# Silu as ScalarE's own function in a fused Mamba and MLP kernel, with a new table of slots

## The reference, cut to what matters

```python
# block 1, on layernorm(x), then added to x
u = rmsnorm(v, norm1_w)
z, x, B, C, dt_raw = split(u @ in_proj_w.T)          # 256, 64, 64, 256, 128 columns
dt = softplus(dt_raw @ dt_proj_w.T + dt_proj_b)
h_t = exp(dt_t * A) * h_{t-1} + (dt_t * x_t) * B_t   # 8 groups x 32 x 32 states, 1024 steps
y = (h . C + x * D) * silu(z);  a = v + y @ out_proj_w.T
a = a + (silu(n @ gate_w.T) * (n @ up_w.T)) @ down_w.T     # n = rmsnorm(a, norm2_w), 704 hidden
# block 2, on layernorm(x), then added to x
x = x + fwht(silu(n @ W1.T) * (n @ W3.T)) @ W2.T           # 1024 hidden
```

## Time and profile before

| | |
|---|---|
| median of three runs | 1240.99 us |
| the profiled execution, its own time | 1238.53 us |
| its span from first to last instruction | 1236.7 us |
| TensorE matmul busy | 1080.3 us (87%) |
| VectorE busy | 1022.8 us (83%), 1161 instructions |
| ScalarE busy | 605.5 us (49%), 1092 instructions |
| GpSimd busy | 925.7 us (75%) |
| mean granted TensorE clock | 0.935 of full speed |

### The profile page before, as it was taken

The page is one execution under the profiler, slowest core; times in us unless marked ns, Lnnn a source line. Parts: engine busy times, 40 slices in busy tenths (PEclk is TensorE's granted clock), DMA queues, the critical chain, the costliest instruction groups (busy, mean ns, idle before and its releaser), DMA issues. The chain is left out here.

```text
span 1236.7 us, 12998 instructions
## 1 busy us (share of the span) xinstructions
PE 1080.3 (87%) x3848; PEld 541.3 (44%) x3848; DVE 1022.8 (83%) x1161; ACT 605.5 (49%) x1092; POOL 925.7 (75%) x564
## 2 busy tenths in 40 slices
PE   2566769999898989999898989999898989898988
PEld 1221224445444454445444554445454544445445
DVE  3378989998898989998899889998999899996222
ACT  3645465545654455545654545545654545443210
POOL 0379998877998788876998788877998799874100
PEclk9676679999999999999999989999999999898889
DMA  5798976774767675774758575674856676550000
GB/s 201 183 248 174 204 174 137 151 165 109 189 137 168 139 180 135 160 164 109 186 126 184 132 175 137 155 167 115 192 132 143 141 187 140 121 109 17 1 0 17
DMA packets 99493, 176.38 MB, mean 143 GB/s; under 512 B 12960, under 2 KB 21600, under 8 KB 98784
## 3 DMA queue, kind: packets, MB, share of 16 engines
q1 hardware_dynamic: 98272, 171.36, 60.7%
q0 software_dynamic: 1152, 4.19, 1.0%
HBM read 150.34 MB, written 8.39 MB: 128 GB/s over the span
## 5 line engine op out<-in xcount | busy, mean ns | idle before, releaser
L959 POOL TENSOR_TENSOR h_s<-h_s,c_s 128x1024 f32<-128x1024 f32 x256 | 604.2, 2362 | 107.6 <-DVE h_s L772 97.6
L546 ACT ACTIVATE p_dt<-p_dt,an_s 128x512 f32<-128x512 f32 x512 | 334.4, 660 | 351.9 <-PE p_dt L408 351.5
L408 PE MATMUL p_dt<-kdt,pick_s 128*128 128x512 f32 x512 | 349.5, 694 | 61.6 <-DVE h_s L772 60.7
L772 DVE TENSOR_TENSOR_SCAN h_s<-p_dt,carry,bt_s 128x512 f32<-128x512 f32 x256 | 321.7, 1273 | 18.2 <-ACT p_dt L546 17.0
L772 DVE TENSOR_TENSOR_SCAN h_s<-p_dt,bt_s 128x512 f32<-128x512 f32 x256 | 305.5, 1213 | 36.5 <-ACT p_dt L546 27.7
L464 PE MATMUL p_r<-nT,w_s 128*128 128x512 f32 x512 | 243.9, 604 | 4.4 <-ACT nT L697 4.4
L939 POOL TENSOR_TENSOR bt_s<-bt_s,b_s 128x1024 f32<-128x1024 f32 x96 | 226.6, 2360 | 19.6 <-DMA bt_s<-dx_rows 19.5
L757 DVE TENSOR_TENSOR bt_s<-bt_s,p_b 128x1024 f32<-128x1024 f32 x160 | 193.1, 1207 | 8.0 <-DMA bt_s<-dx_rows 7.7
L408 PEld LDWEIGHTS p_dt<-kdt,pick_s 128*128 128x128 f32 x512 | 101.5, 202 | 208.8 <-DVE h_s L772 127.4
L453 PE MATMUL p_r<-nT,gu_s 128*128 128x512 f32 x352 | 169.9, 603 | 2.4 <-ACT nT L692 2.4
L419 PE MATMUL p_y<-h_s,ysel_s 128*32 128x512 f32 x1024 | 152.2, 669 | 16.6 <-POOL h_s L959 16.6
(11 more groups left out here) (85 smaller groups left out, 738.6 us busy)
## 6 DMA issues: line engine op xcount, KB each, us to landing
bt_s<-dx_rows SPq DMA_DIRECT2D x512, 256.0 KB, 5.3
kdt<-st_dt SPq DMA_DIRECT2D x64, 128.0 KB, 5.7
tok<-in_x SPq DMA_DIRECT2D x8, 512.0 KB, 7.1
xr_s<-xb_s SPq DMA_DIRECT2D x64, 64.0 KB, 4.0
dx_rows<-dx_s SPq DMA_DIRECT2D x16, 256.0 KB, 5.5
b_s<-xb_s SPq DMA_DIRECT2D x64, 64.0 KB, 5.0
xo<-in_x SPq DMA_DIRECT2D x8, 512.0 KB, 7.3
out<-res POOLq DMA_DIRECT2D x8, 512.0 KB, 6.8
```

The lines of the kernel that those rows point to most:

```text
L408: nc.tensor.matmul(p_dt[DT_BANK[u]][:, :], sel, kdt[:, h, p // 16, :], start=True, stop=True)\
L546: A(p_dt[DT_BANK[u]][:, :], p_dt[DT_BANK[u]][:, :], ACT.Exp, scale=an_s[:, c:c + 1]).then_inc(a_dA, 1)
L772: V.tensor_tensor_scan(h_s[:, u % 8, :], p_dt[DT_BANK[u]][:, :], bt_s[:, u % 16, :], carry[:, u:u + 1] if par else 0.0, ALU.mult, ALU.add) ...
L959: G.tensor_tensor(h_s[:, two, :], h_s[:, two, :], c_s[:, h, :].unsqueeze(1).broadcast_to([P, 2, T]), ALU.mult)\
```

## The change

ScalarE computes silu itself (`ACT.Silu`), so that VectorE's first step of z, gates and W1 falls away, as do the three weight copies; the Walsh-Hadamard transformed W2 gets `scale=2.0` in the copy that it had anyway. The silus of blocks 2k and 2k+1 stand together, one slot after the second of them (`f | 1`); both of z stand one slot after z 1. A bank of z, gate or W1 is now freed by ScalarE. VectorE's product stands two slots after the up or W3 block; for gate 5, which has its up part in the same block, two slots after up 4. The planner is replaced by a written table: for each block its number of steps, its first and its last slot. The order of the blocks changes with it (both gates of a pair come ahead of their ups). Six constants move: `X_SLOT` 58 to 59, `XL_SLOT` 54 to 46, `XO_SLOT` 44 to 41, `KEPT_SLOT` 5 to 3, `DT_STEP` 8 to 0, and the slots of the first half's gating and of the second half's are now named `YG` = 36 and `Y1` = 3, as they were.

```diff
-PLAN = ([("c1", 0, 2, .86)]
-        + [("uT", k, 4, .2) for k in range(2)]
...
-GAP = 5
-AFTER = {("uT", 0): (None, 1), ("out", 0): (None, 3), ("hT", 0): (("out", 1), GAP), ("down", 0): (("gate", GB), 2),
-         ("c0", 0): (("down", 1), 3), ("xT", 0): (("down", 1), GAP)}
+PLAN = [
+    ("c1", 0, 2, 0, 0), ("uT", 0, 4, 2, 3), ("uT", 1, 4, 3, 3), ("dtr", 0, 2, 4, 4), ("out", 0, 4, 4, 4),
+    ("out", 1, 4, 4, 4), ("z", 0, 2, 6, 7), ("z", 1, 2, 8, 9), ("hT", 0, 4, 9, 10), ("xb", 0, 2, 11, 11),
+    ("hT", 1, 4, 11, 11), ("gate", 0, 2, 11, 15), ("gate", 1, 2, 15, 15), ("up", 0, 2, 15, 16),
+    ("up", 1, 2, 16, 17), ("gate", 2, 2, 19, 19), ("gate", 3, 2, 20, 22), ("up", 2, 2, 21, 21),
+    ("up", 3, 2, 23, 23), ("up", 4, 2, 23, 27), ("gate", 4, 2, 24, 24), ("gate", 5, 2, 24, 25),
+    ("dtp0", 0, 1, 28, 29), ("down", 0, 12, 28, 29), ("down", 1, 12, 31, 33), ("c0", 0, 2, 36, 38),
+    ("xT", 0, 4, 37, 38), ("xT", 1, 4, 38, 38), ("w1", 0, 2, 39, 39), ("w1", 1, 2, 39, 42), ("w3", 0, 2, 41, 41),
+    ("w3", 1, 2, 42, 44), ("w1", 2, 2, 42, 44), ("w3", 2, 2, 45, 45), ("w1", 3, 2, 45, 45), ("w1", 4, 2, 47, 49),
+    ("w3", 3, 2, 47, 48), ("w1", 5, 2, 48, 48), ("w3", 4, 2, 48, 48), ("w3", 5, 2, 50, 50), ("w1", 6, 2, 51, 51),
+    ("w1", 7, 2, 51, 51), ("w3", 6, 2, 52, 52), ("w3", 7, 2, 54, 54), ("dtp1", 0, 1, 54, 54),
+    ("w2", 0, 16, 55, 59), ("w2", 1, 16, 59, 61)
+]
...
         for j in range(n):
...
+            s = first + j * (last - first + 1) // n
             slots.setdefault(s, []).append((q, j))
             ends[stage, k] = s
...
-                     "z": (v_zs, 2), "c0": (a_c[0], 1), "c1": (a_c[1], 1), "out": (v_h, 2), "hT": (a_hT, 2),
-                     "gate": (v_ga, GB + 1),
+                     "z": (a_zt, 2), "c0": (a_c[0], 1), "c1": (a_c[1], 1), "out": (v_h, 2), "hT": (a_hT, 2),
+                     "gate": (a_gt, GB + 1),
...
-                A(out_s[:, :, :], out_s[:, :, :], ACT.Copy, scale=0.5).then_inc(w_out, 1)
-                A(down_s[:, 0:GB, :], down_s[:, 0:GB, :], ACT.Copy, scale=0.5).then_inc(w_out, 1)
-                A(down_s[0:64, GB, :], down_s[0:64, GB, :], ACT.Copy, scale=0.5).then_inc(w_out, 1)
...
-                        for k in range(2):
-                            if u == ENDS["z", k] + 1:
+                        if u == ENDS["z", 1] + 1:
+                            for k in range(2):
...
-                                A(zs_s[:, k, :], ring[BANK["z", k]][:, :], ACT.Tanh, scale=0.5).then_inc(a_zt, 1)
+                                A(zs_s[:, k, :], ring[BANK["z", k]][:, :], ACT.Silu).then_inc(a_zt, 1)
...
-                            if u == ENDS["w1", f] + 1:
+                            if u == ENDS["w1", f | 1] + 1:
                                 act.wait_ge(mm["w1"], pt * HB + f + 1)
...
-                                A(th_s[:, f % 2, :], ring[BANK["w1", f]][:, :], ACT.Tanh, scale=0.5)\
-                                    .then_inc(a_ft, 1)
+                                A(th_s[:, f % 2, :], ring[BANK["w1", f]][:, :], ACT.Silu).then_inc(a_ft, 1)
...
-                            if u == ENDS["w1", f] + 2:
+                            if u == ENDS["w3", f] + 2:
                                 dve.wait_ge(a_ft, m + 1)
-                                V.scalar_tensor_tensor(out=th_s[:, f % 2, :], in0=th_s[:, f % 2, :], scalar=1.0,
-                                                       in1=ring[BANK["w1", f]][:, :], op0=ALU.add, op1=ALU.mult)\
-                                    .then_inc(v_fa, 1)
-                            if u == ENDS["w3", f] + 2:
-                                dve.wait_ge(v_fa, m + 1)
                                 dve.wait_ge(mm["w3"], m + 1)
```

More of the change, by code:

```diff
@@ L71 @@
-GAP = 5
-AFTER = {("uT", 0): (None, 1), ("out", 0): (None, 3), ("hT", 0): (("out", 1), GAP), ("down", 0): (("gate", GB), 2),
-         ("c0", 0): (("down", 1), 3), ("xT", 0): (("down", 1), GAP)}
-RING = 3
[L75 to L96, removed]
+PLAN = [
[11 rows of a table added]
+]
@@ L97, in place_steps @@
+RING = 3
+X_SLOT = 59
+XL_SLOT = 46
+XO_SLOT = 41
+KEPT_SLOT = 3
+DT_STEP = 0
+YG = 36
+Y1 = 3
+def place_steps():
+    slots, ends = {}, {}
+    for q, (stage, k, n, first, last) in enumerate(PLAN):
         for j in range(n):
[L98 to L101, removed]
+            s = first + j * (last - first + 1) // n
             slots.setdefault(s, []).append((q, j))
             ends[stage, k] = s
-            at += c
@@ L105, in place_steps @@
[L105 to L110, removed]
+    return slots, ends
+STEPS, ENDS = place_steps()
 BANK = {step[:2]: q % RING for q, step in enumerate(PLAN)}
@@ L187, in build @@
         l_b = [sem(f"l_b{h}") for h in range(2)]
-        w_in, w_gu, w_out, w_an, w_zero, w_pick, w_had, w_w2, w_w2c = (
-            sem(f"w_{n}") for n in ("in", "gu", "out", "an", "zero", "pick", "had", "w2", "w2c"))
+        w_in, w_gu, w_an, w_zero, w_pick, w_had, w_w2, w_w2c = (
+            sem(f"w_{n}") for n in ("in", "gu", "an", "zero", "pick", "had", "w2", "w2c"))
         pe_dt, pe_y = sem("pe_dt"), sem("pe_y")
@@ L203, in build @@
         a_ve, a_kept, a_ms, a_ve2 = (sem(f"a_{n}") for n in ("ve", "kept", "ms", "ve2"))
[L205 to L208, removed]
+        v_bt, v_sc, v_st, v_mv, v_dtl = (sem(f"v_{n}") for n in ("bt", "sc", "st", "mv", "dtl"))
+        v_yf, v_yz, v_h, v_mh, v_x1, v_st2, v_mv2 = (
+            sem(f"v_{n}") for n in ("yf", "yz", "h", "mh", "x1", "st2", "mv2"))
+        v_hd, v_o = sem("v_hd"), sem("v_o")
         g_rr, g_rr2, g_car, g_bt = sem("g_rr"), sem("g_rr2"), sem("g_car"), sem("g_bt")
@@ L364, in _ @@
             freed = {"uT": (a_uT, 2), "dtr": (a_dtr, 1), "xb": (a_xb, 1), "dtp0": (v_dtl, 2), "dtp1": (v_dtl, 2),
[L365 to L367 removed]
+                     "z": (a_zt, 2), "c0": (a_c[0], 1), "c1": (a_c[1], 1), "out": (v_h, 2), "hT": (a_hT, 2),
+                     "gate": (a_gt, GB + 1),
+                     "up": (v_mh, GB + 1), "down": (v_x1, 2), "xT": (a_xT, 2), "w1": (a_ft, HB), "w3": (v_hd, HB),
                      "w2": (v_o, 2)}
@@ L705, in body @@
                                 n = 64 if f == GB else P
-                                A(th_s[0:n, f % 2, :], ring[BANK["gate", f]][0:n, :], ACT.Tanh, scale=0.5)\
-                                    .then_inc(a_gt, 1)
+                                A(th_s[0:n, f % 2, :], ring[BANK["gate", f]][0:n, :], ACT.Silu).then_inc(a_gt, 1)
                         if u == ENDS["down", 1] + 4:
@@ L818, in body @@
                         scan(i, par, u)
-                    if post and u == 3:
+                    if post and u == Y1:
                         gate_y(pt, other, 1)
                         gate_z(pt, other, 1)
[L822 to L828, removed]
                     if pre:
@@ L840, in body @@
                                                 st_dt[:, 0, :].bitcast(F32), ALU.subtract).then_inc(v_dtl, 1)
-                    if units and u == 36:
+                    if units and u == YG:
                         gate_y(i, par, 0)
-                    if units and u == 37:
+                    if units and u == YG + 1:
                         gate_z(i, par, 0)
@@ L880, in body @@
                             n = 64 if f == GB else P
-                            if u == ENDS["gate", f] + 2:
+                            if u == ENDS["up", min(f, GB - 1)] + 2:
                                 dve.wait_ge(a_gt, m + 1)
[L884 to L888, removed]
                                 if f < GB:
```

10 lines of the change are left out of this document (5 added, 5 removed).

## The result

The changed kernel takes 1212.35 us (median of 4 runs, 1211.89 to 1212.90) against 1240.58 us for the kernel before (4 runs): ratio 0.9775, 95% interval 0.9758 to 0.9792. That is 28 us faster. I had forecast faster by 12 us (1229 us): the sign was right, the size less than half, and the time lies outside the forecast's own 1221 to 1237 us, though inside the wide range of 1200 to 1263 us.

What follows compares the result with a forecast made beforehand. TensorE was taken as the bound: a tile is its work plus a few waits. 7 x -1.7 = -11.9 for the tiles and +2.0 for the head gave -9.9, so 1229 us; own range 1221 to 1237, wide range 1200 to 1263.

Steps and rivals of the forecast that it cites:

- What is removed ... is worth about nothing: VectorE loses 128 instructions, 10.7 us a tile, in slots where TensorE is the bound: price 0 by itself.
- longer switch: Rival: ScalarE's pipeline stands empty as long again as each table load, gap 8.4 us: +100, 1340 us; chance 0.03.
- Who waits for the gap: Decays and scans queued behind silu batches come late, 4.5 us a tile on VectorE; covered by TensorE's backlog, so 0.
- What the table moves: TensorE's work stays the same, its waits change in place: sum -1.7 us a tile, bounds -2.7 and +0.7.
- (a): More w2 steps in slots 59 to 61 remove TensorE's 1.89 us wait for scans at slot 62: -2 us a tile.
- (d): After down 1 moves to slot 33, TensorE has little work: the 2.49 us middle wait stays and grows by +1.
- (b): uT moves from slot 1 to slots 2 and 3, cutting waits for L563 and uT copies: -0.9 us a tile.
- (c): hT copies stand behind slot 10's z batch: the wait for hT's input goes, one for its copy comes, +0.2.
- the walk by slots: Bound for the table's effect: walking a tile slot by slot gives 133.7 us, -2.7 a tile.
- Head: With DT_STEP 0, load_dt and load_b go ahead of keep_rows, first drive loads 2 us later: +2.0, bounds 0 and 4.9.
- Late decays: Slower rival: delayed decays cost VectorE 1.5 us a batch, 12 a tile, half reaching the end: 1263 us; chance 0.30.
- packed: Rival: TensorE's waits fall by more than half, minus 5.5 us a tile, 1202 us; chance 0.14.

Runs made afterwards that it cites:

- second filler run: Changed kernel plus 128 extra scalar_tensor_tensor on VectorE, one operand from PSUM, in slots of the old first step, nobody waiting for them: 1223.92 us, ratio 0.9878.
- keep34: Kernel before with keep_rows of the first half in slot 34 and not 30, so load_dt goes ahead of it: 1236.36 us, ratio 0.9974.
- dt8: Changed kernel with DT_STEP back at 8, so load_dt stands in slot 36 behind keep_rows and load_b: 1215.26 us, ratio 0.9816.
- xl54: Changed kernel with XL_SLOT back from 46 to 54: 1212.23 us, ratio 0.9782.

## Why the prediction was right or wrong

The spans differ by 26.6 us where the sum had 9.9. Of the 16.7 us between them 9.3 are in the tiles, 6.1 ahead of tile 1 and 1.3 behind the last scan.

**What bounds: right.** TensorE's busy time is all but the same (2.8 us more in seven tiles) and the gain is in its waits. That was the right ledger to keep.

**"What is removed ... is worth about nothing": the step that failed.** In the new table the removal alone is worth 44.6 us (tanh in both kernels), and 34 us with the loads of Silu counted in. With the price of 0 the sum gave the whole gain to the table: by it the table with the old arithmetic would have come out 10 us faster, and it is 8 us slower. So the forecast's sign was right in part by luck. I priced the removal in the slots of the old order, where TensorE was ahead. The new order asks for banks back sooner (both gates of a pair stand ahead of their ups), and there the stop at VectorE is what TensorE waits for: 30.6 us in the run with the old arithmetic. With the old planner Silu makes the kernel 36 us slower block by block and 55 in pairs; that holds the loads too, and what the removal alone would give there isn't shown. The two halves of the change are of use only together: +8 us for the table, +56 us for Silu in pairs, -28 us for both, by the ratios.

**What ScalarE gains: right.** 146 loads of 1283 ns were forecast and found; ScalarE works 92.2 us in a tile on average, forecast near 95, and VectorE 116.8, forecast near 114. The switch has no more around it than the earlier trace rows showed: in the timeline the z batch is

```profile
590.61 1.28 ACT L579 ACT_TABLE_LOAD   x1
591.91 1.09 ACT L579 ACTIVATE zs_s<-p_r 128x512 f32<-128x512 f32 x2
593.01 1.28 ACT L523 ACT_TABLE_LOAD   x1
594.30 0.66 ACT L523 ACTIVATE p_dt<-p_dt,an_s 128x512 f32<-128x512 f32 x1
```

3.7 us from load to exponential, the 3.66 of the sum. By that the longer switch of the Trainium skill (ScalarE: Activation LUTs, What ACT_TABLE_LOAD costs) isn't borne out by this trace: 1.30 us a switch, not 2.66.

**Who waits for the gap: right in kind, put too low.** I took 0 for the end and found 10.2 us, 1.5 us a tile. The estimate of 4.5 us a tile on VectorE seems to fit, since its wait for decays rose by 30.2 us, 4.3 a tile. That is luck: the run without loads has 53.6 us of it, so 12.3 us, 1.8 a tile, belong to the loads. The other 17.9 us go with a lighter VectorE, which is ahead more often: in the second filler run, with all the loads and VectorE's 86 us back, the wait in seven tiles is 25.9 us.

**What the table moves: -1.7 us a tile forecast, -3.1 measured.** This is the table together with the removal; the table alone makes a tile 1.8 us longer. Scans, items (a) and (d): -1.0 forecast, -0.8 measured, but not by these two alone. In tiles 2 to 6 the wait of about 2 us at slot 62 is gone, as (a) said. The middle wait is 1.8 to 2.1 us (2.5 before), where (d) said it would grow by 1. And four short waits for scans are new in the first 22 us of a tile, 1.4 to 1.8 us together, which no item had. That the sums agree is luck. Two of the tile's waits, from the timeline of TensorE:

```profile
586.66 0.50 PE L388 MATMUL p_dt<-kdt,pick_s 128*128 128x512 f32 x1 [0.52 <-DVE h_s L747]
...
642.26 0.50 PE L388 MATMUL p_dt<-kdt,pick_s 128*128 128x512 f32 x1 [1.77 <-DVE h_s L747]
```

uT, item (b): -0.9 forecast; the copies alone gave 5.4 us, 0.8 a tile, and with the waits for normalised tokens of L563, gone but for 1.6 us of L540, -1.1. hT, item (c): +0.2 forecast; its input's wait fell by 6.8 and its copy's rose by 2.9 us, -0.6. Not in the sum at all: the xT copies ahead of W1 (4.4 us, gone) and the gating of z ahead of out (4.2 to 1.0 us), together -1.1 a tile. I left them out as small; they are more than a third of the 21.2 us. The items add up to -3.5 a tile, and TensorE's busy time grew by 0.4. Of my two bounds the walk by slots (-2.7) was the nearer.

**Head: wrong sign.** +2.0 was forecast, -4.1 measured up to tile 1, of which 3.1 are there at the first scan. Two errors. dtp0 has one step, which stands in the first slot of its range, 28 and not 29, so `keep_rows` is in slot 34, where it stands ahead of `load_b`. And I took the start of the drive loads to hang on the landing of `keep_rows`, where SyncE's own issues were the bound (39.98 + 2.50, tok 0.58, then 43.20). In the changed kernel they go 3.1 us earlier, not 2 later:

```profile
40.12 5.71 SPq L260 DMA_DIRECT2D bt_s<-dx_rows  x12
```

The runs keep34 and dt8 show that the order alone moves the start of tile 1 by 5 to 6 us in either kernel, more than the 4.1 gained, and the end by 3 to 5. The traced run xl54, which has the same head as the changed kernel, starts tile 1 at 173.2 and not 171.8 us, so a difference of 1 us there is within what executions differ by.

**Late decays and packed, the rivals.** The slower rival has a threshold beside it: one more pair of loads in each batch costs 139 us. In the changed kernel it isn't crossed (VectorE waits 9.4 us a tile for decays, the sign of being wrong stood at 12). That late scans alone make up those 139 us isn't shown; they are 30 of the 93 us of TensorE's new waits there. The rival's own sum was off: half of 12 us less the table's 1.7 is 4.3 a tile, and 3.3 only with the 2.7 of the walk by slots. "Packed" asked for 5.5 us a tile; even without loads it is 4.7.

## What to carry to other kernels

A step that leaves an engine's queue is to be priced in the order that the new kernel has, not in the old one: here the same change of arithmetic, loads included, costs 55 us in the old order of blocks and gains 34 us in the new one. When one engine is busy all the time, list every wait that it still has, the small ones too, and go through the change wait by wait. What a table load costs depends on how many stand in one gap: here the first pair in a batch cost 0.2 us, a second pair 2.4 of its 2.8 us, though that pair also held a bank longer. And a wait that grows with a change isn't yet its price: VectorE's wait for decays grew by 30 us, and without the loads 18 of them were still there.

## What was not expected of the hardware

A VectorE instruction with both inputs and its output in SBUF took 659 to 2832 ns beside GpSimd's work, the same with one input in PSUM 673 ns on average. In the timeline of that run two of them take 4.68 us, and the next GpSimd product 2.81 us where 2.36 is its usual time. Behind the last scan, where GpSimd has next to nothing to do, the same instruction takes 0.66 to 0.70 us. The Trainium skill (SBUF — State Buffer, Who interferes with whom) says that a VectorE instruction with two SBUF inputs contends with a GpSimd instruction that reads SBUF; these numbers agree. So 206 us (128 of 1610 ns on average) were added where 86 were meant, and 121 us to the end.
